# Hybrid transformer block on one core: second PSUM banks and other slots at both ends of the schedule

## The chip, the cores and the metric

The kernel runs on one core of a Trainium2 chip. The time is device microseconds of one execution. Six queues matter here: PE (TensorE, its weight loads shown apart as PEld), DVE (VectorE), ACT (ScalarE), POOL (GpSimd), and SP (SyncE), which issues all DMAs. Each works through its own instructions in program order and waits on semaphores for the others.

## The reference

The input x is 8 batches of 512 tokens of width 128, float32. Four sublayers follow each other, each with a layer norm ahead of it and a residual behind it:

```
x = x + causal_attention(ln(x))      # 16 heads of 8, ALiBi, biases
x = x + ffn(ln(x))                   # 128 -> 384 -> 128, silu(gate) * up, int weights / 127
x = x + attention_b(ln(x))
x = x + ffn(ln(x))                   # the same weights

attention_b: scores = softmax(q k^T * scale)             # 16 heads, 512 x 512
             importance of a token = -0.4 entropy + 0.3 maximum + 0.3 influence (column sums)
             51 tokens of the highest importance + 64 compressed groups of 8 tokens = 115 keys
             out = softmax(q k_cat^T * scale) v_cat, then @ Wo
```

So the second attention computes full score matrices only to choose 51 tokens, and then attends to 115 keys ("small attention").

## The kernel before, in words

**Slots.** The order of all work is written out by hand. Time is cut into slots; each engine runs a loop over the slots (L596 for SP, and so on), and in each slot does the steps that fall into it. A step of batch b has a number `a`, and stands in slot FIRST + 64 b + a (`own_slots`, L584). A slot has no length of its own: it takes what its work and its waits take, and an empty slot takes nothing.

**The main tiles.** From slot 170 to slot 681 every slot has one full-score tile of the second attention, 64 per batch, 512 in all: one matmul on PE into bank 0 or 1 (`full_scores`, L1360), the negated copy with row maxima on DVE (L1143), the exponential with its sum on ACT (L882), a threshold on POOL (L720), the entropy sum on DVE (L1042), and every fourth tile the column sums on PE (`influence`, L1368). All other steps of all batches are spread over these slots.

**Ahead of the main tiles (slots 0 to 169)** the constants are made and weights are transposed in a block of its own (L276 to L416). The second block can start on no engine before all engines have ended the first; its last SP step is a wait for the fourteen DMAs of constant rows (L307). Then batch 0 and batch 1 go through the causal attention. Its steps, with `a`: x loaded (-42), statistics (-39), transposes (-34), projections (-32, -28), their bf16 parts stored to DRAM (-22) and reloaded as stacks in two halves (-12, 8); 40 first tiles (`causal_scores`, L1275, a = 0 to 39), whose row maxima DVE takes (`causal_maxima`, L977); these maxima are transposed (23, 43), split into parts by ACT and POOL, and stored and reloaded as rows (27, 47); 40 second tiles (`causal_minus_max`, L1305, a = 31 to 70, four gangs of ten), which ACT exponentiates (L860) into pT; `weigh` (L1328) multiplies them with the values. All first tiles use bank 3 and all second tiles bank 4, so PE writes a tile, waits until the reader has read it, and writes the next. Output projection, norm, the first ffn (a = 79 to 104), the second attention's projections (F_Q at 113, F_K at 115), their store (120) and reload (122, 130) follow; the main tiles of that batch begin at a = 128.

**Behind the main tiles** (a = 192 is the end of batch 7's) stand, per batch: the column of importances (198), the row (202), the picking of tokens (209); the key parts are made (211 to 214) and stored (215), the small key stack and small query stack are loaded (K_LOAD 221, S_QLOAD 223; L642 to L657), both after a wait for the last small second tile of the batch before; 16 small first tiles (`small_scores`, a = 232 to 247, bank 3), their maxima on DVE (L993), transposed (250) and reloaded as rows (254); 16 small second tiles (`small_minus_max`, from a = 263 in gangs of four, one gang in six slots, bank 4), exponentials on ACT into the four tiles p2 (L869), which must wait until the gang before has been weighed (`small_weigh`, L1350); transposes, output projection (294, 300), norm (307, 313), second ffn (315 to 328) and the store (330).

Layer norm is statistics on DVE (`stats`, L967), the inverse root and the normalisation on POOL (`inverse_root` L677, `normalise` L683, four instructions at L690), four transposes on PE (`ln`, L1255). Banks 7 and 2 are handed out in turn to all uses that have no bank of their own; bank 5 takes weighted heads, bank 6 the column sums.

## Time and profile before

| what | value |
|---|---|
| median of three runs | 1777.08 us (1765.18 to 1785.22) |
| the profiled execution | 1775.59 us, its span 1773.8 us |
| ahead of the first full tile | 299.4 us |
| 512 main tiles | 299.4 to about 1619 us |
| behind them | about 155 us |
| busy, share of the span | PE 77%, DVE 71%, ACT 58%, POOL 30% |

The span is what the profile covers; the profiled execution's own time lies 1.8 us above it. A slice's digit in the page is the busy share of one fortieth of the span in tenths. Three lines of the page show the three stages: DVE is at 8 to 9 tenths in the middle only, and the granted clock of PE (PEclk, in tenths of 2.4 GHz) is at 5 in many slices at both ends.

```
PE   1377797788768878888888888887888788787565
DVE  1330432996788798989897989798878789877221
PEclk9555556577758776978797879788877768857566
```

### The profile page before, as it was taken

What the parts mean: (1) busy time and instruction counts of PE and PEld (TensorE: products, weight loads), DVE (VectorE), ACT (ScalarE), POOL (GpSimd) and SP (SyncE); (2) the same over time, 40 slices, a digit from 0 to 9 for tenths busy, and PEclk for the clock granted to TensorE, in tenths of its full rate; (3) what the DMA queues carried; (4) which work ended last, traced back from release to release, by engine and by line L of the source; (5) the groups of instructions that cost most, each with busy time, mean ns of one, the idle gap of its engine ahead of it and who ended that gap; (6) DMA issues with size and microseconds to landing.
All of it is one profiled execution on the core that took longest, in us unless ns stands there. A gap on an engine that the chain in (4) does not pass through costs nothing.

```text
span 1773.8 us, 26884 instructions
## 1 busy us (share of the span) xinstructions
PE 1368.7 (77%) x7981; PEld 607.2 (34%) x7981; DVE 1266.5 (71%) x3771; ACT 1021.9 (58%) x2550; POOL 535.6 (30%) x964
## 2 busy tenths in 40 slices
PE   1377797788768878888888888887888788787565
PEld 0132343234233333443344334433443242243232
DVE  1330432996788798989897989798878789877221
ACT  1024145577547766867586768676777657745132
POOL 3020232254124522442334234423341334212021
PEclk9555556577758776978797879788877768857566
DMA  2201103102302220223023201220111102100100
GB/s 53 45 19 26 25 25 79 24 2 58 69 3 48 49 64 3 48 56 62 5 46 62 57 11 41 62 50 16 24 38 32 24 7 63 19 12 15 24 14 6
DMA packets 69881, 61.39 MB, mean 35 GB/s; under 512 B 12088, under 2 KB 67432, under 8 KB 69736
## 3 DMA queue, kind: packets, MB, share of 16 engines
q1 hardware_dynamic: 69736, 59.68, 16.4%
q8 instruction: 64, 1.05, 0.3%
q14 instruction: 81, 0.66, 0.1%
HBM read 41.19 MB, written 18.27 MB: 34 GB/s over the span
## 4 chain that ended last, share of the span: by engine, by line
PE 38%; DVE 26%; issue 13%; ACT 11%; DMA 4%; POOL 4%; SPq 1%; DVEq 0%; ACTq 0%; POOLq 0%
DVE junk L1042 7%; PE bank L1373 5%; ACT setup L882 4%; PE bank L1273 4%; PE bank L1337 4%; DVE negs L1143 3%; PE bank L1315 3%; PE bank L1398 3%; DVE nm L982 2%; PE bank L1293 2%; ACT pT L860 2%; DVE nml L988 2%; PE bank L1365 2%; DMA k_stacks<-part_dram 2%; PE bank L1408 2%
## 5 line engine op out<-in xcount | busy, mean ns | idle before, releaser
L882 ACT ACTIVATE setup<-negs,nmB 128x512 f32<-128x512 f32 x512 | 367.0, 717 | 235.6 <-DVE negs L1143 224.4
L720 POOL TENSOR_TENSOR thr<-nmB,lnZ 128x1 f32<-128x1 f32 x512 | 150.1, 293 | 880.8 <-ACT lnZ L886 872.3
L1042 DVE SCALAR_TENSOR_TENSOR junk<-negs,thr,setup 128x512 f32<-128x512 f32 x512 | 410.0, 801 | 0.8 <-POOL thr L720 0.5
L1143 DVE TENSOR_SCALAR_CACHE_REDUCE negs<-bank 128x512 f32<-128x512 f32 x512 | 349.5, 683 | 35.8 <-PE bank L1365 35.2
L860 ACT ACTIVATE pT<-bank 128x512 f32<-128x512 f32 x320 | 188.6, 589 | 193.6 <-PE bank L1323 192.8
L1365 PE MATMUL bank<-k_stacks,q_stacks 48*128 48x512 bf16 x512 | 234.6, 464 | 30.8 <-DVE negs L1143 18.9
L1315 PE MATMUL bank<-q_stacks,k_stacks 55*128 55x384 bf16 (+3 forms) x512 | 149.5, 358 | 65.3 <-ACT pT L860 65.2
L1373 PE MATMUL bank<-setup,rz 128*1 128x512 f32 x1024 | 189.6, 824 | 1.5 <-DVE rz L1161 1.5
L982 DVE TENSOR_REDUCE nm<-bank 128x4 f32<-128x512 f32 x128 | 87.8, 686 | 98.8 <-PE bank L1289 98.8
L1293 PE MATMUL bank<-k_stacks,q_stacks 52*128 52x384 bf16 (+2 forms) x384 | 97.0, 344 | 64.1 <-DVE nml L989 45.6
L994 DVE TENSOR_REDUCE nm<-bank 128x4 f32<-128x460 f32 x128 | 81.1, 634 | 81.1 <-PE bank L1408 81.0
L869 ACT ACTIVATE p<-bank 115x512 f32<-115x512 f32 x128 | 75.2, 588 | 82.9 <-PE bank L1416 45.6
L1285 PE MATMUL bank<-k_stacks,q_stacks 52*128 52x128 bf16 x512 | 63.3, 259 | 72.6 <-DVE nm L982 34.3
L1337 PE MATMUL bank<-pT,vA 128*9 128x512 f32 (+3 forms) x1024 | 117.4, 564 | 0.0
L988 DVE TENSOR_REDUCE nml<-bank 128x1 f32<-128x384 f32 x128 | 70.7, 552 | 62.5 <-PE bank L1293 62.4
L886 ACT ACTIVATE lnZ<-Z 128x1 f32<-128x1 f32 x512 | 103.9, 203 | 16.1
L690 POOL TENSOR_SCALAR xn<-x,mv,rstd 128x128 f32<-128x128 f32 x128 | 112.3, 885 | 0.5
L882 ACT ACTIVATION_READ_ACCUMULATOR setup<-negs,nmB 128x1 f32 x512 | 96.7, 189 | 0.0
L1323 PE MATMUL bank<-maskr,maskw 64*128 64x128 bf16 (+1 forms) x640 | 95.1, 234 | 0.0
L1408 PE MATMUL bank<-kcst,s_stacks 48*128 48x115 bf16 x512 | 59.2, 250 | 45.2 <-DVE nm L994 33.4
L1315 PEld LDWEIGHTS bank<-q_stacks,k_stacks 55*128 55x128 bf16 x512 | 37.6, 100 | 160.4 <-ACT pT L860 119.1
L1365 PEld LDWEIGHTS bank<-k_stacks,q_stacks 48*128 48x128 bf16 x512 | 50.7, 101 | 114.6 <-DVE negs L1143 62.3
(195 smaller groups left out, 2424.1 us busy)
## 6 DMA issues: line engine op xcount, KB each, us to landing
part_dram<-part SPq DMA_DIRECT2D x16, 768.0 KB, 3.6
q_stacks<-part_dram SPq DMA_DIRECT2D x192, 64.0 KB
k_stacks<-part_dram SPq DMA_DIRECT2D x192, 64.0 KB
s_stacks<-part_dram SPq DMA_DIRECT2D x48, 128.0 KB
x<-in_L_attn_a_x_dram SPq DMA_DIRECT2D x16, 256.0 KB, 2.9
x_dram<-x SPq DMA_DIRECT2D x8, 256.0 KB, 2.2
x<-x_dram SPq DMA_DIRECT2D x8, 256.0 KB, 2.7
out_dram<-x SPq DMA_DIRECT2D x8, 256.0 KB, 2.5
```

The source lines that it names most:

```text
L690: last = pool.tensor_scalar(xn[:, t, :], xs[u][:, t, :], mv[u][:, t, 0:1], rstd[u][:, t:t + 1], ALU.subtract, ALU.mult)
L720: pool.tensor_tensor(thr[mb % 2][:, h, t:t + 1], nmB[mb % 2][:, h, t:t + 1], lnZ[mb % 2][:, h, t:t + 1], ALU.subtract).then_inc(s_bt, 1)
L860: act.activation(pT[:, js[0]:js[0] + len(js), c * T:c * T + WIDTH[c]], bank[4][:, :].rearrange("p (j q) -> p j q", j=len(js)), ACT.Exp).th ...
L882: act.activation(E[:, n % NE, :], negs[n % NS][:, :], ACT.Exp, scale=-1.0, bias=nmB[mb % 2][:, h, t:t + 1], accum_out=Z[mb % 2][:, h, t:t ...
L982: last = dve.tensor_reduce(nm[0][:, :, h], bank[3][:, :].rearrange("p (t k) -> p t k", t=NT), AX_X, ALU.max, negate=True)
L1042: dve.scalar_tensor_tensor(out=junk[:, :], in0=negs[n % NS][:, :], scalar=thr[mb % 2][:, h, t:t + 1], in1=E[:, n % NE, :], op0=ALU.min, op ...
L1143: dve.tensor_scalar(negs[n % NS][:, :], RING[n % RN][:, :], -1.0, None, ALU.mult, ALU.min, accum_out=nmB[mb % 2][:, h, t:t + 1]).then_inc( ...
L1293: last = pe.matmul(ps[:, at_:at_ + t * P], qst[0][0:A_SC, h, t * P:(t + 1) * P], kst[0][0:A_SC, h, 0:t * P], start=True, stop=True)
L1315: pe.matmul(ps[:, first:first + w], kst[0][0:A_MX, h, j * P:(j + 1) * P], qst[0][0:A_MX, h, j * P:T], start=not squares, stop=True, skip_g ...
L1337: last = pe.matmul(bank[5][QROWS * j:QROWS * j + HD + 1, k * P:T], vA[:, k, HPQ * g + j, :], pT[:, j, c * T + at_:c * T + at_ + T - k * P] ...
L1365: pe.matmul(RING[n % RN][:, :], qst[1][0:B_SC, h, t * P:(t + 1) * P], kst[1][0:B_SC, h, :], start=True, stop=True).then_inc(s_bs, 1)
L1373: last = pe.matmul(INFL[QROWS * t:QROWS * t + 1, :], rz[mb % 2][:, h, t:t + 1], E[:, (NT * h + t) % NE, :], start=(h == 0), stop=(h == H - 1))
```

## The change

Five things, all in the order and the places of work; nothing that is computed changes.

1. Batch 0's x is loaded by the first DMA of the first block, and SP no longer waits at that block's end for the constant rows; PE waits for them ahead of the first causal tile.
2. The first tiles of batches 0 and 1 alternate between banks 3 and 0, and the second tiles of slots below 176 between banks 4 and 1 (the full-score tiles wait for their last readers). The small first and second tiles of batches 5, 6 and 7 alternate between banks 3 and 4, and their exponentials have a second set of four places (pT, by then free), so a gang no longer waits for the one before to be weighed.
3. FIRST is 52 and the front steps (x load to the second rows) are numbered apart: batch 0's front stays in the slots where it was, everything else comes ten slots later, so the main tiles stand in slots 180 to 691. Relative to the main tiles all steps of batches 1 to 4 stay where they were.
4. Late steps move relative to the main tiles' end. Batch 5: second small tiles two to a slot, and everything from the output projection on ten slots earlier. Batch 6: small first tiles 30 to 23 slots ahead of the end (before: 24 to 9 ahead), small second tiles from 10 ahead to the end itself (before: 7 to 28 behind it). Batch 7: the slots stay; its small query stack is loaded at M_END + 4, ahead of the picking.
5. The normalisation runs on DVE for (norm, batch) = (0, 0), (1, 0), (2, 0) and (3, 7).

The order of uses within a slot is now also by batch and step, in the table of banks and in the waits that look up an earlier use (`last_before`, `ahead`). S_X2, the reload of x for the last residual, moves from 270 to 292.

```diff
-        s_full = {k: sem(f"bank{k}_uses_written") for k in (2, 3, 4, 7)}
-        s_free = {k: sem(f"bank{k}_uses_read") for k in (2, 3, 4, 5, 7)}
+        s_full = {k: sem(f"bank{k}_uses_written") for k in (0, 1, 2, 3, 4, 7)}
+        s_free = {k: sem(f"bank{k}_uses_read") for k in (0, 1, 2, 3, 4, 5, 7)}
...
+                sp.dma_start(xs0[:, :, :], x[0].rearrange("(t p) d -> p t d", p=P)).then_inc(s_xin, DMA)
...
-                sp.wait_ge(s_rows, (2 * AL + 6) * DMA)
...
-        FIRST = 42
-        X_LOAD = -42
-        P_STATS = -39
-        P_TURN = -34
-        P_Q, P_K = -32, -28
-        P_STORE = -22
-        P_HALF = (-12, 8)
+        FIRST = 52
+        FRONT = -1000
+        HEAD_START = 10
+        X_LOAD = FRONT - 42
+        P_STATS = FRONT - 39
+        P_TURN = FRONT - 34
+        P_Q, P_K = FRONT - 32, FRONT - 28
+        P_STORE = FRONT - 22
+        P_HALF = (FRONT - 12, FRONT + 8)
         P_V = 24
-        A1_AT = 0
-        A_JOIN = (21, 41)
-        A_TMAX = (23, 43)
-        A_ROWS = (27, 47)
+        A1_AT = FRONT
+        A_JOIN = (FRONT + 21, FRONT + 41)
+        A_TMAX = (FRONT + 23, FRONT + 43)
+        A_ROWS = (FRONT + 27, FRONT + 47)
+        FRONT_END = FRONT + 60
         A2_AT = (31, 41, 51, 61)
         WEIGH = tuple(A2_AT[g] + (6, 10, 12)[c] for g in range(NG) for c in range(3))
         X_AGAIN = 47
...
         M_END = M_AT + NMAIN
         R_COL, R_ROW, R_PICK = M_END + 6, M_END + 10, M_END + 17
         K_PARTS = R_PICK + 2
-        K_LOAD, S_QLOAD = 221, 223
+        K_LOAD = 221
+        S_QLOAD = (223,) * (B - 1) + (M_END + 4,)
         V_PLACE = 228
         S1_AT = 232
         S_TMAX = 250
         S_ROWS = 254
         S2_AT = tuple(263 + 6 * g for g in range(NG))
-        S_X2 = 270
+        S_X2 = 292
         S_OUT, S_PROJ, S_STATS, S_LNT = 294, 300, 307, 313
         S_GATE, S_UP, S_DOWN = (315, 317, 319), (321, 323, 325), 328
         S_STORE = 330
         SLOTS = FIRST + NMAIN * (B - 1) + S_STORE + 2
+        LATE = B - 3
+        ALONE = ((0, 0), (1, 0), (2, 0), (3, B - 1))
+        def slot(b, a):
+            if a < FRONT_END:
+                a -= FRONT + (0 if b else HEAD_START)
+            elif b == B - 3 and a >= S2_AT[0]:
+                a = S2_AT[0] + 2 + (a - S2_AT[0]) // 2 if a < S_OUT else a - 10
+            elif b == B - 2 and V_PLACE - 4 <= a < S_OUT:
+                a = (V_PLACE - 4 + (a - V_PLACE + 4) // 4 if a < S1_AT else V_PLACE - 2 + (a - S1_AT) // 2
+                     if a < S_TMAX - 2 else a - 14 if a < S_ROWS + 1 else 241 + (a - S_ROWS) // 2 if a < S2_AT[0]
+                     else 246 + (a - S2_AT[0]) // 2)
+            return FIRST + NMAIN * b + a
...
             for u in range(N1):
-                use(3, z + A1_AT + u, "a1", b, u)
+                use((3, 0)[u % 2] if b < 2 else 3, b, A1_AT + u, "a1", b, u)
             for u in range(N2):
-                use(4, z + A2_AT[u // G2] + u % G2, "a2", b, u)
+                a = A2_AT[u // G2] + u % G2
+                use((4, 1)[u % 2] if slot(b, a) < FIRST + M_AT - 4 else 4, b, a, "a2", b, u)
             for h in range(H):
-                use(3, z + S1_AT + h, "s1", b, h)
-                use(4, z + S2_AT[h // HPQ] + h % HPQ, "s2", b, h)
+                use((3, 4)[h % 2] if b >= LATE else 3, b, S1_AT + h, "s1", b, h)
+                use((3, 4)[h % 2] if b >= LATE else 4, b, S2_AT[h // HPQ] + h % HPQ, "s2", b, h)
...
+        def small_room(b, h):
+            return pT[:, h % HPQ, 0:T] if b >= LATE and h // HPQ % 2 else p2[h % HPQ][:, :]
+        steps_of = {g: [] for g in range(SLOTS + 1)}
+        for b in range(B):
+            for a in (*range(X_LOAD, FRONT_END), *range(P_V, S_STORE + 2)):
+                steps_of[slot(b, a)].append((b, a))
...
-                        if a == S_QLOAD:
+                        if a == S_QLOAD[b]:
                             if b:
-                                sp.wait_ge(s_full[4], count("s2", b - 1, H - 1))
+                                sp.wait_ge(s_full[at("s2", b - 1, H - 1)], count("s2", b - 1, H - 1))
...
-                                if NG * b + h // HPQ:
-                                    act.wait_ge(s_pv[1], NG * b + h // HPQ)
-                                act.wait_ge(s_full[4], count("s2", b, h))
-                                act.activation(p2[h % HPQ][0:NK, :], bank[4][0:NK, :], ACT.Exp).then_inc(s_free[4], 1)
+                                gone = NG * b + (max(0, h // HPQ - 1) if b >= LATE else h // HPQ)
+                                if gone:
+                                    act.wait_ge(s_pv[1], gone)
+                                if b == LATE and h == HPQ:
+                                    act.wait_ge(s_pv[0], 3 * NG * B)
+                                bk = at("s2", b, h)
+                                act.wait_ge(s_full[bk], count("s2", b, h))
+                                act.activation(small_room(b, h)[0:NK, :], bank[bk][0:NK, :], ACT.Exp
+                                               ).then_inc(s_free[bk], 1)
...
+                def normalise(u, b):
+                    dve.wait_ge(s_rs[u], b + 1)
+                    other = last_before(("ln", u, b), *(("ln", v) for v in range(4)))
+                    if other:
+
+                        dve.wait_ge(s_full[at(*other)], count(*other))
+                    for t in range(NT):
+                        last = dve.tensor_scalar(xn[:, t, :], xs[u][:, t, :], mv[u][:, t, 0:1], rstd[u][:, t:t + 1],
+                                                 ALU.subtract, ALU.mult)
+                    last.then_inc(s_xn[u], 2)
...
+                            if a == STATS[u] + 2 and (u, b) in ALONE:
+                                normalise(u, b)
...
+                    if b == 0 and u == 0:
+                        pe.wait_ge(s_rows, (2 * AL + 6) * DMA)
...
                     if n >= RN:
                         pe.wait_ge(s_bm, n - RN + 1)
+                    else:
+
+                        pe.wait_ge(s_free[n], written[n])
```

## Rows read from the trace of the kernel before

**Rows 1.** Timeline, first 56 us: start us, us, engine, line, operation, count, [idle <-releaser]
```profile
19.29 0.59 SPq L305 DMA_DIRECT2D kcst<-setup  x1
...
24.47 0.87 DVE L970 BATCH_NORM_STATS2 st<-x 128x6 f32<-128x128 f32 x4 [11.63 <-DMA x<-in_L_attn_a_x_dram]
...
27.26 3.14 POOL L690 TENSOR_SCALAR xn<-x,mv,rstd 128x128 f32<-128x128 f32 x4
...
55.33 0.61 PE L1285 MATMUL bank<-k_stacks,q_stacks 52*128 52x128 bf16 x4 [19.30 <-DMA k_stacks<-part_dram]
```

**Rows 2.** Timeline, batch 0's first tiles: starts of two successive groups of five.
```profile
63.26 0.61 PE L1285 MATMUL bank<-k_stacks,q_stacks 52*128 52x128 bf16 x4 [0.78 <-DVE nml L985]
...
71.20 0.61 PE L1285 MATMUL bank<-k_stacks,q_stacks 52*128 52x128 bf16 x4 [0.79 <-DVE nml L985]
```

**Rows 3.** Timeline, a first tile with another tile right behind it.
```profile
118.00 0.60 PE L1285 MATMUL bank<-k_stacks,q_stacks 52*128 52x128 bf16 x4
...
118.83 0.63 PE L1315 MATMUL bank<-q_stacks,k_stacks 55*128 55x384 bf16 x2
```

**Rows 4.** Timeline, batch 0's second tiles: same place of two successive gangs.
```profile
139.29 1.90 PE L1337 MATMUL bank<-pT,vA 128*9 128x512 f32 x8
...
156.93 1.89 PE L1337 MATMUL bank<-pT,vA 128*9 128x512 f32 x8
```

**Rows 5.** Waits of PE, 107:169.5, then 169.5:299.4: us in total, times, longest.
```profile
PE bank L1315 <- ACT pT L860: 11.5, 15, 1.7
...
PE bank L1315 <- ACT pT L860: 8.2, 14, 1.7
PE bank L1293 <- DVE nml L989: 5.0, 8, 0.8
PE bank L1285 <- DVE nm L982: 4.3, 4, 1.9
PE bank L1365 <- DMA k_stacks<-part_dram: 2.9, 1, 2.9
```

**Rows 6.** Timeline at L1273, and tile negs: first and last start.
```profile
272.62 1.13 PE L1273 MATMUL bank<-xnT,wqb 128*128 128x512 f32 x2
...
L1143 DVE TENSOR_SCALAR_CACHE_REDUCE negs<-bank x512: 673/683/693, 299.4 to 1613.3; 128x512 f32<-128x512 f32 x171
```

**Rows 7.** Windows: length, PE, PEld, DVE, ACT, POOL busy, PEclk, DMA, GB/s.
```profile
240.00:260.00 20.00, 19.14 (x79) 10.58 (x78) 6.69 (x13) 5.48 (x10) 3.98 (x4) 0.53 0.00 1
...
1500.00:1619.10 119.10, 94.25 (x437) 37.91 (x435) 104.00 (x327) 77.67 (x216) 27.64 (x69) 0.70 0.09 15
```

**Rows 8.** Timeline behind the last main tile, to batch 7's small scores.
```profile
1624.25 0.88 DVE L1070 TENSOR_SCALAR diag<-identf,imp 128x128 f32<-128x128 f32 x4
1624.55 4.27 PE L1398 MATMUL bank<-wdT,gated 128*128 128x128 f32 x24
...
1646.21 0.34 SPq L641 DMA_DIRECT2D kcp_dram<-kcp  x1
...
1655.59 2.11 SPq L648 DMA_DIRECT2D kcst<-kcp_dram  x6
...
1657.75 2.15 SPq L655 DMA_DIRECT2D s_stacks<-part_dram  x6
...
1670.96 0.54 PE L1408 MATMUL bank<-kcst,s_stacks 48*128 48x115 bf16 x4 [8.92 <-DMA s_stacks<-part_dram]
```

**Rows 9.** Timeline, batch 7's small scores: a reader; the transposes behind them.
```profile
1674.13 0.64 DVE L994 TENSOR_REDUCE nm<-bank 128x4 f32<-128x460 f32 x1 [0.66 <-PE bank L1408]
...
1693.43 1.06 PE L1301 MATMUL bank<-identf,nm 128*16 128x128 f32 x4
```

**Rows 10.** Timeline, batch 7: two successive gangs' weighting; the final normalisation.
```profile
1721.78 1.90 PE L1356 MATMUL bank<-p,vsm 115*9 115x512 f32 x8
...
1729.50 1.90 PE L1356 MATMUL bank<-p,vsm 115*9 115x512 f32 x8
...
1748.83 3.13 POOL L690 TENSOR_SCALAR xn<-x,mv,rstd 128x128 f32<-128x128 f32 x4
```

135 lines of the change are left out of this document (70 added, 65 removed).

## The prediction

> **What bounds the kernel now.** I read the busy slices first: DVE is full only between 299 and 1619 us, so the kernel has three stages, a head of 299 us, 512 main tiles, and 155 us behind them. The windows come next: in the late main part DVE is busy for 104 of 119 us and PE for 94 of them at a granted clock of 0.70 [rows 7]. There a wait that is taken from PE is worth little, since DVE sets the pace. The timelines of head and end show the opposite: two engines hand one bank to and fro and neither is full. A group of five first tiles takes 7.94 us [rows 2], a gang of second tiles 17.64 us [rows 4], a gang of small second tiles 7.72 us [rows 10]. The list of PE's waits says what ends them: the reader of the one bank, ACT or DVE [rows 5]. The change works on these two ends.
>
> **The start.** Now SP issues its last constant DMA until 19.9 us, waits for them, the block ends, and only then x is fetched; statistics begin at 24.47 us [rows 1]. Afterwards x is long there and the block ends when SP has issued, so they begin at about 20.4 us: 4.0 us less. The x load ahead of the weights costs them one issue of some 0.4 us, which is hidden because SP's constant rows end the block. Four normalisations on POOL take 3.14 us [rows 1]. The nearest DVE row is four 128x128 tensor-scalar instructions in 0.88 us [rows 8]: 2.2 us less. Together 6.2 us; bounds 2 and 8.
>
> **Batch 0 and 1's first tiles.** With two banks PE writes one while DVE reads the other. A diagonal tile then costs PE about 0.95 us at this clock (0.83 to the next tile's first matmul where nothing waits [rows 3], and a little for the mask's end), the wider ones are bound by DVE's reads, about 0.85 and 0.7. A group of five: 2 x 0.95 + 2 x 0.85 + 0.7 = 4.3 us instead of 7.94. The bounds are 3.8 (DVE's reads alone) and 7.94. Batch 0's 40 tiles start at 55.3 - 6.2 = 49.1 us and take 8 x 4.3 + 3.1 for the value projection and one transposition of maxima: 86.6. The transposes of batch 1's norm now stand right behind (slot 82, five slots behind its statistics); that norm stays on POOL and is late by about 2.5 us, so the second tiles start at about 90 us. The rows of the first maxima are loaded some 13 us behind slot 65 and are there by then, which is what the ten slots of head start are for.
>
> **Second tiles.** A gang of ten takes 17.64 us [rows 4]. PE waited 11.5 us for ACT over some three gangs [rows 5], and each such wait also delays what its queue holds behind; I take 13.5 us per gang, bounds 11 and 17.6. To batch 1's first tile (three tiles into the fourth gang): 3 x 13.5 + 2.5, and 5.1 for two projections and a transposition, so 90 + 48 = 138 us. That tile now starts at 169.5 us: 31.5 us less, the start's 6.2 included. From there to the second attention's first projection at 272.62 us [rows 6] PE waits 9.3 us for DVE in the two largest lines, and of 8.2 us for ACT about half lies ahead of that point [rows 5]. Of these 13 us I count 11, since norm (1, 0) puts a wait for POOL's inverse root into DVE's queue, with batch 1's maxima behind it and PE behind them. Banks 0 and 1 cost the full tiles nothing: their last other readers have been done for several slots.
>
> **From 272.6 us to the first full tile** nothing is won. It is a chain of projection, parts on ACT and POOL, store, and reload of the stacks, and PE already waits 2.9 us for the last DMA [rows 5]. It keeps its 26 us. Whatever PE saves in these slots ends in that wait. Head: 31.5 + 11 = 42.5 us.
>
> **The main tiles.** Ten empty-looking slots are only renumbered. But batch 6's small second tiles (16 tiles, four weightings, four turns) and the end of batch 5's ffn now run beside full tiles. DVE gets about 5 us more (four times norm_four, three hidden products, a residual); PE gets 16 x 0.5 + 4 x 1.5 + 4 x 0.9 + 4.3 = 22 us in some 25 slots where it had (119 - 94) / 119 = 21% idle [rows 7], 12 us in 58 us. Bounds 5 (DVE alone) and 22 (all of PE's). Nearer the first, since DVE is the fuller engine: **+9 us**. SP's loads of batch 6's query stack keep their place, a wait for batch 5's last small tile; the main tiles wait no more than now.
>
> **Behind them.** From the end, 1619.1 us [rows 7], to batch 7's first small scores at 1670.96 us it takes 51.9 us. In this stretch PE does batch 5's down projection (4.27 us) between the diagonals and the row of importances; the key parts are stored at 1646.21, but their load waits until 1655.59 for batch 6's last small second tile, and the query stack goes behind it and lands 11 us after its last issue [rows 8]. Afterwards: 5 us for the last gang of batch 6, column, diagonals and row 4.3, ranks and choice 5.7, picking and copies 4.2, parts 2.1, the store 2.0, the key load's six issues 2.1 and its landing, taken as 4 (bounds 2, the other DMAs' landing, and 11, the query's): 29.4 us. The query stack is loaded beside the ranks. That is 22.5 us less. Batch 7's small scores to the transposes: 22.5 us now; with DVE's reads of 0.64 us [rows 9] on two banks 16 x 0.67, 2 for the projection and statistics between, and 3 for batch 6's norm on POOL, which is now late and stands ahead of those transposes: 15.5, so 7 us less. Small second tiles: a gang is 4 tiles of 0.6, a weighting of 1.90 and a turn of 1.1 on PE, and 0.3 for a wait, 5.7 instead of 7.72 us [rows 10], since it no longer waits for the old gang's places. Three gangs and 1.5 in the first: 7.5 us less. The final norm on DVE: 3.13 us [rows 10] become 0.9: 2.2 less. Sum behind the main tiles: 39 us.
>
> **Sum.** -42.5 + 9 - 39 = -72.5. Three more places take waits that I did not cost (batch 1's second stack half, the first ffn's norms, the order of ACT): +3.5. So -69 from the execution's 1775.6 us gives 1706.6; the median lies 1.5 us above that execution, so **1708 us**.
>
> **A rule against the trace.** PE's clock: between 240 and 260 us PE is busy 19.1 of 20 us, and the granted clock is 0.53 [rows 7], nearly the lower of its levels, 1.2 GHz. I therefore price both ends at 1.2 GHz, and denser tiles alone change nothing. The Trainium skill (TensorE: Matmul & The Clock Gate, Part 1) says that the gate opens to 2.4 GHz once the engine has been busy. By that rule the denser head would run at the upper level; the trace so far speaks against it.
>
> **Rivals.** *The clock opens (12%).* For: the granted clock does rise at times at the ends. Against: row of 240 us. The second tiles' gangs and the first tiles' matmuls would lose about a third of PE's time: some 20 us more, 1688 us. *The main tiles pay (20%).* For: PE at 1.2 GHz there has just 12 us of idle time for 22 us of work, and a small tile that waits for ACT blocks the full-score matmul behind it in the same queue. Then the main part gets longer by 25 to 30 us instead of 9: 1726 us. *Transfers set the head's pace (18%).* Each stack half is issued in 4 us and lands some 6 us later, maxima rows take 12 us from transposes to landing; slots are now shorter by a third. If two or three of these come late the head gives back 20 us: 1728 us. *The second bank does nothing (3%)*, because hand-over and in-order waits are the cost and not the bank: what is left is the start, the earlier loads and the norms, -6 - 22.5 - 2 + 9: 1754 us. *Slower (3%).* The turn of banks 7 and 2 and the waits looked up by `last_before` now follow (slot, batch, step). If in the main slots two uses of one slot changed places against PE's order, each batch would get a wait that DVE feels. It decides from 69 / 8 = 8.6 us per batch on; at 10 us per batch it gives 1787 us. One weighting, 1.9 us, is the longest thing that such a wait would stand behind, so it would take five of them per batch. The forecast itself has 44%, its own range 1692 to 1722.
>
> **Numbers.** The range 1686 to 1742 takes in the forecast with its bounds, the two dearer rivals and most of the clock's. Under 1% of a change can't be told from none here. Faster by over 1% (below 1759) are all cases but the slower one and some of the useless bank: 0.93; within 1% 0.04; slower 0.03.
>
> **What would show it.** In the changed trace: statistics at about 20.4 us; a group of five first tiles in about 4.3 us; a gang of second tiles in 13 to 14 us; batch 1's first tile near 138 us and the first full tile near 256 us, with a DMA wait of 3 to 5 us ahead of it; from the first full tile to the last entropy sum about 1329 us; then 29 us to batch 7's small scores, whose reads follow each other at 0.67 us; gangs of small tiles at 5.7 us. The forecast is wrong if the head ends later than 270 us (transfers), if the main part exceeds 1340 us (moved work), or if the clock in the head is well above 0.6.

## The result and the profile after

| | before | after |
|---|---|---|
| median, same chip | 1775.13 us (1765.18 to 1785.22, 4 runs) | 1674.01 us (1659.50 to 1683.65, 4 runs) |
| ratio | | 0.942, 95% interval 0.933 to 0.952 |
| profiled execution, its span | 1775.59, 1773.8 us | 1659.50, 1657.7 us |
| up to DVE's first full tile | 299.4 us | 226.5 us |
| main tiles | 1319.7 us | 1328.4 us |
| behind them | 154.7 us | 102.8 us |

The forecast was 1708 us, range 1686 to 1742: the right sign, but too little gain. The changed kernel was run and profiled a second time beside its variants (the run e17_after_again below): 1685.34 us median of 6 (1658.16 to 1693.44), beside 1780.07 us before, span 1684.7. All ten of its times have the median 1681.7; I compare variants with that number, since medians of four and of six runs of one and the same code lie 11 us apart. My medians take all runs, while the ratios with an interval count only the fast ones, those within 1.5% of the fastest of their kernel.

The start, first causal tiles. Timeline: start us, us, engine, line, operation, count, [idle <-releaser]; first profile of the changed kernel.

```profile
20.58 0.87 DVE L1010 BATCH_NORM_STATS2 st<-x 128x6 f32<-128x128 f32 x4 [7.74 <-PEq L276]
...
23.29 1.11 DVE L1024 TENSOR_SCALAR xn<-x,mv,rstd 128x128 f32<-128x128 f32 x4 [1.43 <-POOL rstd L715]
...
49.35 0.58 PE L1343 MATMUL bank<-k_stacks,q_stacks 52*128 52x128 bf16 x4 [19.32 <-DMA k_stacks<-part_dram]
...
53.46 0.60 PE L1343 MATMUL bank<-k_stacks,q_stacks 52*128 52x128 bf16 x4 [0.19 <-DVE nml L1041]
...
57.59 0.60 PE L1343 MATMUL bank<-k_stacks,q_stacks 52*128 52x128 bf16 x4 [0.19 <-DVE nml L1041]
```

They answer to [rows 1, 2]: the first tile 6 us earlier, a group of five in 4.13 us instead of 7.94. Next the weightings of batch 0's gangs, which answer to [rows 4], in the same profile:

```profile
99.19 1.89 PE L1396 MATMUL bank<-pT,vA 128*9 128x512 f32 x8
...
111.85 1.89 PE L1396 MATMUL bank<-pT,vA 128*9 128x512 f32 x8
...
122.70 1.05 PE L1396 MATMUL bank<-pT,vA 128*9 128x512 f32 x8
...
125.80 1.05 PE L1396 MATMUL bank<-pT,vA 128*9 128x384 f32 x16
```

and the same work in its second profile:

```profile
98.46 1.89 PE L1396 MATMUL bank<-pT,vA 128*9 128x512 f32 x8
...
111.13 1.89 PE L1396 MATMUL bank<-pT,vA 128*9 128x512 f32 x8
...
123.49 1.89 PE L1396 MATMUL bank<-pT,vA 128*9 128x512 f32 x8
...
199.44 1.89 PE L1396 MATMUL bank<-pT,vA 128*9 128x512 f32 x8
...
208.53 1.05 PE L1396 MATMUL bank<-pT,vA 128*9 128x384 f32 x16
```

A gang takes 12.66 and 12.67 us while PE is at its lower level, 1.2 GHz (17.64 before). Then the first profile goes to 2.4 GHz at about 120 us: the same weighting takes 1.05 us and the next gang 10.85. In the second every weighting up to 199.44 takes 1.89 us. So one code has two heads, 226.5 and 241.3 us. Windows show the clock (columns as in [rows 7]): first the second profile, then the first.

```profile
100.00:120.00 20.00, 19.66 (x122) 7.81 (x119) 0.55 (x2) 10.60 (x20) 3.83 (x6) 1.00 0.25 74
...
180.00:200.00 20.00, 20.00 (x65) 8.07 (x68) 7.07 (x14) 9.79 (x17) 5.94 (x5) 0.50 0.00 0
200.00:216.00 16.00, 15.02 (x116) 9.18 (x108) 5.49 (x20) 8.25 (x17) 4.35 (x5) 0.80 0.18 67
216.00:228.00 12.00, 10.98 (x92) 6.01 (x92) 0.55 (x2) 10.07 (x21) 6.09 (x7) 1.00 0.39 102
```

```profile
100.00:120.00 20.00, 19.66 (x125) 7.68 (x117) 0.55 (x2) 10.96 (x20) 4.00 (x6) 1.00 0.24 69
...
160.00:188.00 28.00, 27.91 (x86) 10.85 (x88) 10.95 (x23) 12.78 (x22) 11.64 (x12) 0.50 0.01 2
188.00:214.00 26.00, 24.37 (x213) 13.59 (x206) 6.23 (x23) 18.97 (x36) 11.50 (x12) 0.99 0.31 106
```

Two readings. The clock column says 1.00 from 100 to 120 us in both, where the weightings of 1.89 us say 0.5: in the stretch ahead of the first recorded change the column can't be trusted, durations can. And PE busy for 27.91 of 28 us is at 0.50, while 24.37 of 26 us is at 0.99: how full the engine is does not tell the level by itself.

What PE waits for, from batch 1's first tile (132.66 us) to the first full tile (second profile, list of 136 to 241 us, nothing more in the 3 us ahead; us in total, times, longest), beside the second list of [rows 5]:

```profile
PE bank L1428 <- DMA k_stacks<-part_dram: 7.1, 1, 7.1
PE bank L1373 <- ACT pT L895: 2.8, 3, 1.0
PE bank L1315 <- POOL xn L724: 2.7, 1, 2.7
PE bank L1351 <- DVE nm L1034: 1.2, 3, 0.7
PE bank L1373 <- DMA q_stacks<-nm_dram: 1.0, 1, 1.0
PE bank L1343 <- DVE nml L1041: 0.4, 1, 0.4
PE bank L1351 <- DVE nml L1041: 0.4, 1, 0.4
```

The waits for readers fell from 20.9 us (8.2, 5.0 and 4.3 of [rows 5], and two lines of 1.8 and 1.6) to 4.8 us, and the stack's DMA is what PE meets next, 7.1 us instead of 2.9. Behind the main tiles (SP's DMAs, first profile), answering to [rows 8]:

```profile
1554.19 2.50 SPq L689 DMA_DIRECT2D s_stacks<-part_dram  x6
...
1572.40 0.35 SPq L675 DMA_DIRECT2D kcp_dram<-kcp  x1
1574.12 2.10 SPq L682 DMA_DIRECT2D kcst<-kcp_dram  x6
```

and PE there, answering to [rows 9, 10]:

```profile
1579.60 0.93 PE L1471 MATMUL bank<-kcst,s_stacks 48*128 48x115 bf16 x8 [8.41 <-issue]
...
1596.29 1.06 PE L1359 MATMUL bank<-identf,nm 128*16 128x128 f32 x4
...
1619.20 1.04 PE L1416 MATMUL bank<-pT,vsm 115*9 115x512 f32 x8 [0.51 <-ACT pT L908]
...
1622.87 1.04 PE L1416 MATMUL bank<-p,vsm 115*9 115x512 f32 x8 [0.51 <-ACT p L908]
```

The scores of batch 7 start 24.7 us behind the main tiles (51.9 before), the transposes of their maxima 16.7 us later (22.5), and a gang takes 3.67 us (7.72). In the second profile the first two numbers are 25.4 and 16.7, but most gangs run at the lower clock:

```profile
1639.75 1.89 PE L1416 MATMUL bank<-pT,vsm 115*9 115x512 f32 x8 [0.41 <-ACT pT L908]
...
1645.16 1.90 PE L1416 MATMUL bank<-p,vsm 115*9 115x512 f32 x8 [0.41 <-ACT p L908]
```

that is 5.41 us each, and its whole stretch behind the main tiles is 111.9 us instead of 102.8.

### The profile page after: what moved, and what is told of

It reads as the page before. It is cut to its first block, busy times and chain, and to the rows that moved or that the text cites. A ratio compares the mean times of both kernels' runs of the same rounds, so it can differ in the third digit from the quotient of the medians.

```text
span 1657.7 us, 26884 instructions
## 1 busy us (share of the span) xinstructions
PE 1327.9 (80%) x7981; PEld 593.3 (36%) x7981; DVE 1263.1 (76%) x3787; ACT 1018.1 (61%) x2550; POOL 524.5 (32%) x948
## 3 DMA queue, kind: packets, MB, share of 16 engines
q8 instruction: 64, 1.05, 0.3%
## 4 chain that ended last, share of the span: by engine, by line
PE 39%; DVE 23%; issue 13%; ACT 12%; POOL 5%; DMA 4%; SPq 1%; DVEq 0%; ACTq 0%; POOLq 0%
DVE junk L1095 6%; PE bank L1436 6%; PE bank L1329 6%; ACT setup L922 5%; PE bank L1396 3%; PE bank L1461 3%; DVE negs L1196 3%; PE bank L1373 2%; DMA k_stacks<-part_dram 2%; PE bank L1428 2%; ACT pT L895 2%; POOL xn L724 2%; PE bank L1351 2%; DVE nml L1040 2%; PE bank L1343 1%
## 5 line engine op out<-in xcount | busy, mean ns | idle before, releaser
L1196 DVE TENSOR_SCALAR_CACHE_REDUCE negs<-bank 128x512 f32<-128x512 f32 x512 | 349.6, 683 | 39.0 <-PE bank L1428 38.7
L1373 PE MATMUL bank<-q_stacks,k_stacks 55*128 55x384 bf16 (+3 forms) x512 | 141.5, 342 | 55.5 <-ACT pT L895 54.6
L1343 PE MATMUL bank<-k_stacks,q_stacks 52*128 52x128 bf16 x512 | 63.5, 260 | 58.1 <-DVE nm L1034 22.8
L1396 PE MATMUL bank<-pT,vA 128*9 128x512 f32 (+3 forms) x1024 | 107.1, 521 | 0.0
L724 POOL TENSOR_SCALAR xn<-x,mv,rstd 128x128 f32<-128x128 f32 x112 | 98.9, 890 | 0.2
L908 ACT ACTIVATE p<-bank 115x512 f32<-115x512 f32 x104 | 60.7, 587 | 61.1 <-PE bank L1479 41.9
L1381 PE MATMUL bank<-maskr,maskw 64*128 64x128 bf16 (+1 forms) x640 | 91.1, 226 | 0.0
```

The costliest lines, as they stand in the source:

```text
L724: last = pool.tensor_scalar(xn[:, t, :], xs[u][:, t, :], mv[u][:, t, 0:1], rstd[u][:, t:t + 1], ALU.subtract, ALU.mult)
L1196: dve.tensor_scalar(negs[n % NS][:, :], RING[n % RN][:, :], -1.0, None, ALU.mult, ALU.min, accum_out=nmB[mb % 2][:, h, t:t + 1]).then_inc( ...
L1373: pe.matmul(ps[:, first:first + w], kst[0][0:A_MX, h, j * P:(j + 1) * P], qst[0][0:A_MX, h, j * P:T], start=not squares, stop=True, skip_g ...
L1396: last = pe.matmul(bank[5][QROWS * j:QROWS * j + HD + 1, k * P:T], vA[:, k, HPQ * g + j, :], pT[:, j, c * T + at_:c * T + at_ + T - k * P] ...
```

## The experiments

Each starts from the changed kernel unless it says otherwise. Numbers of stretches are from one profile each; whole times are medians.

**Head alone, tail alone.** `e1_head_only`: `LATE = B`, old slots for batches 5 and 6, `S_QLOAD = (223,) * B`, `S_X2 = 270`, no (3, 7) in ALONE.

> The changed kernel with its late part undone: small tiles of all batches on one bank each and in p2 alone, batches 5 and 6 in their old late slots, the query stack and x reload at their old steps, the last norm on POOL. The changed kernel's trace has its first full tile at 226.5 us where the kernel before has 299.4. Theory A (the head gained 73 us in every run): first full tile at 226 to 230 us, main tiles again 1320 us, the part behind them again 155 us, in all 1775 - 73 = 1702 us. Theory B (the head is worth the 42.5 us that I priced, the rest was a lucky clock of the one profiled run): first full tile near 256 us, 1733 us. The two parts are independent if this gain and that of the late part alone add up to 101 us.

`e2_tail_only`:

```diff
-                use((3, 0)[u % 2] if b < 2 else 3, b, A1_AT + u, "a1", b, u)
+                use(3, b, A1_AT + u, "a1", b, u)
...
-                use((4, 1)[u % 2] if slot(b, a) < FIRST + M_AT - 4 else 4, b, a, "a2", b, u)
+                use(4, b, a, "a2", b, u)
...
-        FIRST = 52
-        HEAD_START = 10
-        ALONE = ((0, 0), (1, 0), (2, 0), (3, B - 1))
+        FIRST = 42
+        HEAD_START = 0
+        ALONE = ((3, B - 1),)
```

and x and the wait for the constant rows where they were.

> The changed kernel with its head undone: first and second tiles of batches 0 and 1 on banks 3 and 4 alone, old slots of the front, x loaded in the second block, the wait for the constant rows back at the end of the first block, norms of batch 0 on POOL. Theory A (as the changed kernel's trace reads): main tiles +9 us, behind them 103 us instead of 155, sum -43: 1732 us, and the first full tile at 299 us. Theory B (my pricing: +9, -39): 1745 us. Rival (the late part gains only because of the earlier head, for instance through the clock): over 1755 us.

Beside a kernel before of 1777.91 us: head alone 1722.09 (1690.23 to 1723.17), tail alone 1736.45 (1722.52 to 1756.16). That is 56 and 41 us, in sum 97, against 96 for both together (1777.9 - 1681.7). So close a sum is partly luck: head alone has three times at 1721 to 1723 and one at 1690, and the ratio of tail alone to before, 0.984, has an interval from 0.963 to 1.006. The stretches say it better: head alone is 52.8 us shorter in its span than the kernel before, tail alone 33.2, in sum 86.0, and the second profile of both together 89.1. Within 3 us the two ends are independent. Head alone has its first full tile at 241.8 us, neither theory's number: 57.6 us less, 15 more than I priced, in a profile in which the weightings stay at 1.89 us up to 200 us. Its main part is 1320.0 us, as before. Tail alone has 111.8 us behind the main tiles and 1330.8 in them.

**The banks alone.** `e3_head_one_bank` has the first two edits of the last diff and nothing else; `e4_tail_one_bank` is

```diff
-                use((3, 4)[h % 2] if b >= LATE else 3, b, S1_AT + h, "s1", b, h)
-                use((3, 4)[h % 2] if b >= LATE else 4, b, S2_AT[h // HPQ] + h % HPQ, "s2", b, h)
+                use(3, b, S1_AT + h, "s1", b, h)
+                use(4, b, S2_AT[h // HPQ] + h % HPQ, "s2", b, h)
```

> The changed kernel with only the second banks of the head taken away: first tiles of batches 0 and 1 on bank 3, second tiles on bank 4. Start, ten slots of head start, norms on DVE and the whole late part stay. Theory A (the second banks carry the head's gain): a group of five first tiles 7.5 to 8 us instead of 4.13, a gang of second tiles 17 us instead of 9 to 12.7, first full tile near 287 us (of 73 us only the start's 6 and some 6 for the earlier slots are left), in all 1674 + 61 = 1735 us. Rival (earlier slots and the start carry it, and the clock comes by itself): under 1695 us.

> The changed kernel with only the second banks of the small tiles taken away: small first tiles on bank 3, small second tiles on bank 4, also for the last three batches. Their second room for exponentials, the moved slots, the early query stack and the last norm on DVE stay. Theory A: batch 7's small first tiles take again about 1.3 us each instead of 0.7, 7 us more, and its gangs of small second tiles go from 3.66 to about 6 us, 9 us more: 1674 + 16 = 1690 us. Rival (the second room for exponentials and not the bank shortens the gangs): gangs stay below 4.5 us and the whole costs 5 to 9 us, 1681 us. If batch 6's tiles beside the main tiles are felt as well, the main part exceeds 1340 us.

Without the head's second banks: 1752.01 us (1740.11 to 1765.22, 10 runs), 70 us more, and DVE's first full tile at 301.6 us. That is later than before the change although its first tile starts 6.4 us earlier: the ten slots of head start keep first and second tiles apart, its 40 first tiles take 65.5 us to the first second tile (52.1 before, overlapped; 39.7 with two banks). All of the head's gain hangs on the banks. Without the tail's: 1715.19 us (1705.02 to 1723.01), 33 us more where I expected 16. Behind the main tiles it has 127.1 us, 15 more than the second profile and about what I expected, with gangs of 6.93 us (timeline):

```profile
1669.97 1.89 PE L1416 MATMUL bank<-pT,vsm 115*9 115x512 f32 x8
...
1676.90 1.90 PE L1416 MATMUL bank<-p,vsm 115*9 115x512 f32 x8
```

The rest is in the main part, 1351.0 us instead of 1328 to 1332. This edit takes the second banks from batches 5 and 6 too, whose small tiles stand beside full ones. PE's waits for the reader of small first tiles in the whole main part, all batches (us in total, times, longest), first here, then in the second profile of the changed kernel:

```profile
PE bank L1471 <- DVE nm L1047: 26.6, 40, 2.0
```

```profile
PE bank L1471 <- DVE nm L1047: 17.7, 27, 1.9
```

That is 8.9 us more. In the same lists PE's waits for the reader of small second tiles are 10.6 us instead of 4.8, and those of the full tiles 18.8 instead of 14.8: together 18.7 of the 19.5 us by which this main part is longer than the second profile's.

**Is it the clock?** `e5_before_filler` is the kernel before with one more matmul behind every second tile of the slots ahead of the main tiles:

```diff
+                    pe.matmul(INFL[:, :], identf[:, :], FILL, start=True, stop=True)
```

> The kernel before (single banks) with 72 or more extra matmuls of 128x512 float32 into the idle bank 6, one behind every second tile of the slots ahead of the main tiles. They compute nothing that is used. They fill PE's waits for ACT. Theory 'waits' (the second bank helps because PE no longer waits; a busy PE alone changes nothing): a gang of second tiles stays at 17 us or gets longer, PE's granted clock in it stays at 0.5, and the whole gets 0 to 40 us slower, since a filler of four passes at the lower level costs more than the 0.8 us that PE waits per tile. Rival 'clock' (the denser queue opens the clock, and that is most of what my forecast missed): in the gangs the granted clock goes to 1.0, the weighting of 1.89 us becomes 1.05, and a gang gets shorter than 17 us.

1774.19 us (1762.85 to 1803.86, 10 runs) beside 1779.84: no difference. Its second tiles (timeline):

```profile
150.81 1.05 PE L1342 MATMUL bank<-pT,vA 128*9 128x512 f32 x8
151.79 0.39 PE L1316 MATMUL bank<-q_stacks,k_stacks 55*128 55x384 bf16 x2
...
152.22 1.13 PE L1331 MATMUL bank<-identf 128*128 128x512 f32 x2
153.28 0.39 PE L1316 MATMUL bank<-q_stacks,k_stacks 55*128 55x256 bf16 x2
...
168.43 1.05 PE L1342 MATMUL bank<-pT,vA 128*9 128x512 f32 x8
```

Each theory is right in one half: the clock did open, every full weighting from 131 to 308 us takes 1.05 us (none stands between 200 and 244 us, where the granted clock is 0.50), and yet a gang takes 17.62 us (and 19.46 the one ahead), no less than at the lower clock. But this does not show what the higher clock is worth with one bank. Ten fillers of 1.13 us are 11.3 of these 17.62 us, and PE is busy for all of the 40 us from 150 to 190:

```profile
150.00:190.00 40.00, 40.00 (x216) 14.76 (x215) 3.90 (x10) 14.03 (x24) 1.69 (x4) 1.00 0.12 28
```

So the fillers took up both the old waits and what the clock saved. In its profile the head is 310.6 us, 11 longer than before, and the main part 1312.4, 7 shorter. What one bank does at the higher clock stands in the kernel before itself, for a few tiles of batch 1 (timeline of second tiles, first at the lower level, then at the upper):

```profile
144.25 0.60 PE L1315 MATMUL bank<-q_stacks,k_stacks 55*128 55x256 bf16 x2 [0.75 <-ACT pT L860]
...
145.82 0.60 PE L1315 MATMUL bank<-q_stacks,k_stacks 55*128 55x512 bf16 x1 [0.75 <-ACT pT L860]
...
258.85 0.39 PE L1315 MATMUL bank<-q_stacks,k_stacks 55*128 55x256 bf16 x2
...
260.10 0.39 PE L1315 MATMUL bank<-q_stacks,k_stacks 55*128 55x512 bf16 x1 [0.75 <-ACT pT L860]
```

From tile to tile it takes 1.57 us at the lower level and 1.25 at the upper, and the wait for ACT is 0.75 us in both. So the clock shortens PE's own part and leaves the hand-over as it is; the second bank removes the hand-over. With one bank the higher clock pays less, but it does pay.

`e12_fill_waits` puts fillers into the changed kernel: five such matmuls ahead of the first full tile, four ahead of batch 7's scores, two ahead of its last transposes.

> The changed kernel plus eleven extra matmuls of 128x512 float32 into idle bank 6 that compute nothing used: five in PE's 7.3 us wait ahead of the first full tile, four in the 8.4 us wait ahead of batch 7's small scores, two in the 4.8 us wait ahead of the last transposes. In the run with fillers among the second tiles of the kernel before such a matmul took 2.07 us at the lower clock and 1.13 us at the upper, so each group fits into its wait. Theory A (the tail's time depends on the clock, and a PE that works through its waits keeps or gets the upper one): batch 7's gangs of small tiles take 3.7 us, the last down product 2.9 us, granted clock in the two stretches behind the fillers 1.0, part behind the main tiles 96 to 103 us in every run instead of 103 to 111; median 1664 us. Rival (the clock is given by something else, the fillers change nothing or delay): gangs 5.4 us, down 4.3 to 5.5 us, 1674 to 1680 us.

Measured 1686.62 us (1671.59 to 1696.60): nothing won. The tail does run as foretold, 101.9 us with gangs of 3.66 us, but so does the changed kernel's first profile without fillers (102.8), and in the stretch right behind the four fillers the clock is low again (window, columns as before):

```profile
1600.00:1617.00 17.00, 11.39 (x79) 7.66 (x76) 11.19 (x25) 0.41 (x1) 4.38 (x6) 0.53 0.00 1
```

So the fillers did not hold the clock there, and Theory A is not shown.

**The moved slots.** `e6_late_slots_old` takes the two branches for batches 5 and 6 out of `slot`.

> The changed kernel with batches 5 and 6 back in their old late slots; the second banks, the second room for exponentials, the early query stack and the last norm on DVE stay. Theory A (the moved slots shorten what stands ahead of batch 7's small scores): main part 1320 us instead of 1328, end of the main tiles to batch 7's small scores 40 us or more instead of 22 to 25, since batch 5's down projection and batch 6's small tiles stand there again; sum +15 to +25 us: 1695 us. Rival (DMAs set that stretch anyway, the load and store of key parts and stacks): under 30 us there, and the whole at or below 1674, as the main part gives back 8 us.

1689.04 us (1681.68 to 1700.18). From the end of the main tiles to batch 7's scores 47.2 us, as in Theory A, and 133.8 us in all behind them, 22 more than in the second profile. But the main part did not get its time back (1335.3 us, within the 1326 to 1340 of the other profiles with the late part, e4, e13 and e16 left out). The whole is only 7 us slower; its profile has a head of 221.3 us, shorter by a clock that was up at 98 us already. The stretch is shown, the whole not settled.

**The query stack's load.** `e9_qload_old`: `S_QLOAD = (223,) * B`.

> The changed kernel with batch 7's small query stack loaded at its old step, behind the key stack, and not beside the ranks. In the changed kernel the key load is issued at 1574.1 us and the scores start at 1579.6. Theory A (the query load, issued 2.1 us long behind the key load and landing about 9 us after its start, sets the scores' start): 3 to 8 us later, main-tile end to batch 7's small scores 28 to 33 us instead of 22 to 25, 1679 us in all. Rival (the key load's own landing is the limit and both land together): within 1.5 us.

1701.37 us (1693.25 to 1711.89), 20 us more, and 37.6 us from the end of the main tiles to the scores, 12 to 13 more. Timeline of SP and PE:

```profile
1590.37 2.12 SPq L682 DMA_DIRECT2D kcst<-kcp_dram  x6
1592.53 2.15 SPq L689 DMA_DIRECT2D s_stacks<-part_dram  x6
```

```profile
1607.65 0.93 PE L1471 MATMUL bank<-kcst,s_stacks 48*128 48x115 bf16 x8 [20.44 <-DMA s_stacks<-part_dram]
```

The scores start 13 us behind the end of the query load's last issue, and in the changed kernel 3.4 us behind that of the key load (1576.22 to 1579.60). The two loads are not of one size: six issues of 128 KB, and six of 28.8 KB. I had expected 3 to 8 us; this one line is worth more than what I priced for all the norms on DVE.

**The smaller parts.** `e11_no_head_start`: `FIRST = 42`, `HEAD_START = 0`.

> The changed kernel without the ten slots of head start of batch 0: its second tiles begin in slot 73 beside its last nine first tiles, as before the change. Everything else of the change stays. My prediction's view (the head start lets the maxima's rows arrive): second tiles start some 10 us later than the first tiles alone would allow, because the 12 us from the transposed maxima to the landing of the rows are not covered by four tiles of 0.83 us; first full tile 5 to 12 us later than in the changed kernel: 1682 us. Rival (without the head start first and second tiles overlap, DVE and ACT work side by side, and the head gets shorter): 0 to 8 us faster, 1669 us. The run with the head's single banks and with the head start had its second tiles at 114.4 us where the kernel before has 107.4, so the overlap is worth something with single banks.

1684.73 us (1672.49 to 1703.85). The second tiles start 34.1 us behind the first (39.7 with the head start), batch 1's first tile 76.8 us behind, where two profiles with head start and an equally early rise of the clock have 74.1 and 74.1. Worth 3 us at most; whole times do not tell.

`e13_one_room`: `small_room` returns `p2[h % HPQ]` always, and ACT waits for the gang before.

> The changed kernel without the second set of four places for the small exponentials: p2 alone, so ACT waits until the gang before is weighed, as before the change; the two banks stay. Measured so far for batch 7's gangs: single banks and two rooms 6.9 us, two banks and two rooms 5.4 us at the lower clock and 3.67 at the upper, all single 7.7. Theory A (the room takes only the last 0.8 us of the old gang): gangs of 6.0 to 6.5 us at the lower clock, 2 to 3 us on batch 7's tail, the whole 1677 us. Rival (room and bank only help together, since ACT waits for the weighing anyway): gangs of 7.5 us, and batch 6's tiles beside the main tiles lengthen these by 5 us or more: 1687 us.

1679.27 us (1658.22 to 1681.48): no loss in the whole. Gangs of 5.76 us at the lower clock instead of 5.41. The main part was 1348.9 us, as the rival says, but the head 215.9; with one profile I can't say that the 17 us belong to the room.

`e14_start_norms_old`: x load, wait for the rows and all norms as before.

> The changed kernel with x fetched in the second block again, SP's wait for the constant rows at the end of the first block, and all normalisations on POOL. My pricing: 4.0 us for the start, 2.2 for the first norm, 2 for the head's other one and 2.2 for the last: first causal tile at 55.5 us instead of 49.4, batch 1's first tile 6 us later, last norm 3.1 us instead of 1.1; in all 1674 + 9 = 1683 us. Rival (the delay at the start ends in the 7.3 us wait for the stack ahead of the first full tile): first full tile less than 3 us later and 1677 us in all. I hold the first: that wait follows the projections by a fixed chain.

First causal tile at 56.1 us (48.3 to 52.1 in the 13 profiles with the new start), batch 1's first tile 74.1 us behind it as in e13: the start's 6 us hold at their place. The whole, 1679.26 us (1669.57 to 1695.03), does not show them.

`e7_turn34` gives banks 3 and 4 in turn to all tiles that had one:

```diff
+            if k == "t":
+                k = (3, 4)[small % 2]
+                small += 1
```

> The changed kernel with banks 3 and 4 handed out in turn to all small and causal tiles of all batches that have one bank now, so that in the main part too a tile need not wait for its direct forerunner's reader. In the changed kernel PE and its loads wait for such readers (lines of second tiles, first tiles, small tiles) some 300 us in sum within the main part, beside full tiles that DVE bounds. Theory A (DVE is the bound in the main part; its 104 busy us of 119 leave 12%): main part 1328 - 10 to -40 us. Rival (each such wait is hidden, or the turn makes a second tile wait for a first tile's reader): within 10 us of 1674 or slower. My own number: 1660 us.

1672.51 us (1660.19 to 1690.10), main part 1336.1 us: the rival, as far as one profile tells. `e15_more_norms` puts (0, 1), (1, 1), (2, 1) and (3, 6) on DVE too, and `e16_norms_turn` joins both edits; `e17_after_again` is the changed kernel, on the same chip.

> The changed kernel with four more normalisations on DVE: batch 1's first three and batch 6's last. In the changed kernel PE waits 2.1 us for POOL's normalisation ahead of batch 0's second tiles and 2.3 us ahead of batch 6's last norm's transposes. Theory A (both waits are on the path): second tiles start 2 us earlier after the first tiles (38 us instead of 39.7), the maxima's transposes of batch 7 also 2 us earlier relative to its first small score (14.7 instead of 16.7), sum 4 to 6 us, 1670 us. Rival (what waits is the chain of projections and loads behind, and DVE's four reads delay the maxima): no change in either stretch.

> The same with banks 3 and 4 handed out in turn to all small and causal tiles as well. The turn alone gave 1672.5 us beside a kernel before of 1779.8. Theory A (the turn is worth some 5 us in the main part, the norms 5 more): 1665 us. Rival (DVE bounds the main part and the turn does nothing): as e15 within the runs' spread.

> The changed kernel itself once more, so that its parts are seen in a second profile and it shares a chip with the next two. Theory A (waits are gone in every run, the clock's rises come by chance): a1 at 49 to 50.5 us, batch 1's first tile between 121 and 136 us according to when the weighting drops from 1.89 to 1.05 us, first full tile between 220 and 241, main part 1326 to 1340, end of the main tiles to batch 7's small scores 22 to 25 us, gangs 3.7 us at the upper or 5.4 at the lower clock, median 1665 to 1690. Rival (the first profile's head of 226.5 us and tail of 103 us belong to the kernel): the same within 3 us.

e15: 1684.22 us (1669.17 to 1695.91) against 1685.34; the two stretches shrink by 1.0 us (39.7 to 38.7) and 1.1 us (16.7 to 15.6), half of what was expected. e16: 1666.58 us (1664.68 to 1688.87), ratio to before 0.941 (0.936 to 0.947) against 0.937 (0.930 to 0.944) for the changed kernel: its median is 19 us lower, its interval is not. Its profile has the shortest main part of all with the late part, 1318.1 us, where e7 with the same turn of banks has 1336.1; one profile of each does not settle what the turn is worth. No version is shown to beat the changed kernel.

## Why the prediction was wrong

The second profile (e17) has the lower clock at most of the places where I assumed it; with the first it splits the error.

| us | foretold | second profile | first profile |
|---|---|---|---|
| head | -42.5 | -58.1 | -72.9 |
| main tiles | +9 | +11.8 | +8.7 |
| behind them | -39 | -42.8 | -51.9 |
| allowance | +3.5 | | |
| sum | -69 | -89.1 | -116.1 |

The second profile beats the forecast by 20.1 us: 15.6 in the head and 3.8 behind the main tiles, less 2.8 in them, and the allowance of 3.5, for which no run shows a cause. Of the 15.6 us, 0.5 lie at the start, 4.9 in the tiles up to batch 1's first, 8.1 from there to the first projection, 2.1 behind it. The first profile's further 27 us are for the most part the clock at both ends (below).

**Start: right.** Statistics at 20.58 us (20.4), first tile at 49.35 (49.1). The norm is 1.11 us on DVE, not 0.9.

**First and second tiles: right, slightly dear.** Group 4.13 us (4.3), second tiles at 89.03 (90), gang 12.66 us at the lower clock (13.5). From the first causal tile to batch 1's first it takes 84.0 us in four profiles without an early rise (88.9 foretold, 114.2 before). The bank is the cause: e3 has 125.8.

**Batch 1's first tile to the first projection: the step that failed.** I took 11 us from 103.1; it is 84.0 in the second profile and 81.3 in three others of the same head. That is 19 us and more, because the term priced PE's waits and nothing else. Windows of PE over this stretch (columns as in [rows 7]), before and in the second profile:

```profile
169.52:272.62 103.10, 87.06 (x400) 40.41 (x398) 40.18 (x100) 29.98 (x52) 25.95 (x29) 0.55 0.10 22
```

```profile
132.66:216.67 84.01, 78.07 (x399) 40.15 (x398) 40.49 (x108) 29.56 (x52) 19.66 (x21) 0.82 0.12 26
```

PE's idle time falls from 16.0 to 5.9 us: 10.1, my 11. Its busy time falls from 87.1 to 78.1 us for the same matmuls: 9 us that I had put at nothing. (The second clock is not to be trusted; a part of it lies ahead of the first recorded change.) The stretch splits at the weighting of batch 1's first gang. Up to there it takes 79.5 us before and 66.8 in the second profile, nearly all at the lower level in both, and 8.0 of the 12.7 us are idle time. Behind it the clock counts for more than the waits:

```profile
249.03:272.62 23.59, 20.54 (x122) 11.27 (x121) 5.66 (x18) 9.58 (x17) 7.83 (x10) 0.65 0.14 49
```

```profile
199.44:216.67 17.23, 16.25 (x121) 9.59 (x121) 6.05 (x22) 9.17 (x17) 4.72 (x6) 0.79 0.16 62
```

Only 2.1 of these 6.4 us are idle time; 4.3 are the same matmuls in less busy time at a higher granted clock. In the first profile and in e1, e4 and e7 it is 14.5 us, in the first with 13.47 us busy at 0.96. Before, the clock was up for some 7 of these us only (the full weighting at 260.48 us takes 1.05, the one at 270.31 again 1.89 us); now it is up at the first weighting (e13) or rises within some 9 us of it. In six of the first eight profiles of the table below it then stays up. In the other two, e9 and e13, one full weighting in between is at 1.89 us again, and the stretch takes 19.7 and 15.3 us.

Not all of the 9 us is the clock. In a gang of batch 0 whose weightings take 1.89 us in both, busy time falls too, 13.14 to 12.44 us of PE (windows 139.29:156.93 before, 98.46:111.13 in the second profile), probably because the ends of matmuls in the profile are modelled, and an end that the next matmul overlaps adds no busy time. And e3 has 101.4 us from batch 1's first tile to the first projection, 15.5 idle and 85.8 busy: without the second banks neither part is won, although behind the weighting its granted clock is 0.75. Whether the denser queue raises the clock or only lets a raised clock pay stays open. My reading of [rows 5] was off as well: ahead of the projection the waits for ACT are 3.1 us, not half of 8.2, and the two smaller lines for DVE (1.8 and 1.6 us) were left out.

**From there to the first full tile: right.** 24.6 us (26 kept, 26.7 by the same measure before), with the DMA wait grown to 7.1 us (3 to 5). What PE saved in these slots did end in that wait. The rival of slow transfers took nothing back.

**Main tiles: right.** +8.7 and +11.8 (+9). The price hangs on the second banks of the small tiles: e4 has +31.

**Behind them: right in kind, 4 us short at the lower clock.** 25.4 us to batch 7's scores (29.4): the scores start 3.4 us behind the key load's issues (4), and batch 6's last gang is over before the main tiles end and costs nothing, not 5. Scores to transposes 16.7 (15.5), gangs 5.41 (5.7). What my text treated as one line, the query stack beside the ranks, is 12 to 13 us of this by e9.

**The clock: the second thing that failed.** I priced both ends at the lower level and set the rule of the upper aside. My argument was one row: PE busy 19.1 of 20 us at 0.53 [rows 7]. It is true, and the later rows repeat it (27.91 of 28 us at 0.50). But it shows that a busy PE can stay at the lower level, not that it must. Where the engine does rise, a gang goes from 12.66 to 9.03 us (122.70 to 131.73) and from 5.41 to 3.67, and a run gains 15 us in the head and 9 behind the main tiles. That is the "some 20 us more" to which I gave 12%; it is not there in every run but in some, so it belonged into the range and not into a rival. Heads with the same instructions:

| profile | full weighting first at 1.05 us | batch 1's first tile behind the first causal tile | first full tile on PE |
|---|---|---|---|
| e1, e4, e7, e17 | 207 to 209 us | 84.0 us | 238.5 to 241.2 |
| e9 | 137 | 83.6 | 235.8 |
| first of the changed kernel | 123 | 79.5 | 225.8 |
| e13 | 111 | 74.1 | 215.3 |
| e6 | 98 | 71.8 | 220.7 |
| e12, the same up to its fillers at 232 us | 97, then all at 1.89 up to 198 | 82.8 | 239.8 |

The Trainium skill (TensorE: Matmul & The Clock Gate, Part 1) says that the point of the rise differs from run to run. The trace agrees, and here it is up to 26 us of head for one code of the head. The same page puts the cost of the ramp under 1% of a typical kernel and advises against fitting it; in this kernel, where the clock rises and falls many times, head and tail together move by 24 us in 1680, 1.4%, between the two profiles of the changed kernel.

The mean clock of a run does not give its time: in the second set 0.785 goes with 1684.2 and 1693.4 us and 0.756 with 1658.2. So that these rises explain the spread of the whole times is likely from two profiles, not shown. What decides whether PE rises at 98 or at 208 us, and whether it stays up (e12 against e6), stays open.

## What to carry to other kernels

A stage in which two engines hand one buffer to and fro is worth somewhat more than its waits. At one and the same clock level a gang went from 17.64 to 12.67 us, 5.0 less, while PE's idle time in it fell by 4.3. Between batch 1's first tile and the main tiles the listed waits for readers fell by 16 us and the time by 21, but there a part is the clock. Price such a stage at both clock levels when the trace shows both for one instruction, and put the difference into the range. Before placing a load behind another on a queue, ask which of them could have gone earlier: one moved load was worth 12 to 13 us at its place.

## What the runs showed that I had not expected

- One code, one chip, 1658 to 1693 us: the spread of a single-core kernel is here as large as most parts of the change. Stretches of a profile told what medians of four could not.
- A matmul of 128x512 float32 takes 2.07 us at the lower clock and 1.13 at the upper, and in e5 PE was busy for 10.00 of 10 us at 0.50 (110 to 120 us) as at 1.00 (130 to 140).
- Extra matmuls that only fill waits raised the clock in the profiled head of the old kernel (weightings 1.89 to 1.05 us). That head was 11 us longer for it, and the whole time no different, 1774 against 1780 us.
- The scores could start 3.4 us behind the last issue of a stack load of six times 28.8 KB, but 13 us behind one of six times 128 KB.
